# Attention on one core: TensorE takes two score tiles, then the transposes of two tiles, then values

## The reference

```python
scores = jnp.einsum('bqhd,bkhd->bhqk', q, k) * scale
attn = jax.nn.softmax(scores, axis=-1)
out = jnp.einsum('bhqk,bkhd->bqhd', attn, v)
...
x = _layernorm(x + _L0_attn_ref(x, ...))
x = _layernorm(x + _L0_ffn_ref(x, ...))
```

## Time and profile before

| | us |
|---|---|
| median of 3 runs | 987.49 |
| lowest and highest | 984.86, 988.55 |
| the profiled execution | 981.67 |
| its span, first to last instruction | 980.0 |
| TensorE busy in it | 918.8 |
| ScalarE, VectorE, GpSimd busy | 680.4, 633.7, 672.0 |

### The profile page before, as it was taken

One profiled execution on the slowest core, in us unless ns is written; L12 is line 12 of the kernel. 1 busy time (PEld: TensorE's weight loads), 2 busy tenths in 40 slices (PEclk: granted clock), 3 DMA queues, 4 the chain that ended last, 5 costly groups with the idle time before them and its releaser, 6 DMA issues.

```text
span 980.0 us, 17588 instructions
## 1 busy us (share of the span) xinstructions
PE 918.8 (94%) x5110; PEld 637.5 (65%) x5110; DVE 633.7 (65%) x1008; ACT 680.4 (69%) x1140; POOL 672.0 (69%) x503
## 2 busy tenths in 40 slices
PE   6799899999999999979989989999999999998985
PEld 3558666666666666658776866666666666666874
DVE  1665677777776677744457667777777777773455
ACT  3735988888878888851334598888878888875132
POOL 0007788988888989760341778889898988875034
PEclk9999999999999999999999999999999999999998
DMA  9834798888787887999000579888787787889201
GB/s 254 260 156 113 141 167 156 147 152 152 150 155 144 152 152 145 160 177 346 16 25 23 129 140 165 149 156 158 144 159 148 147 152 150 151 155 194 118 1 43
DMA packets 419814, 142.24 MB, mean 145 GB/s; under 512 B 405596, under 2 KB 413616, under 8 KB 418736
## 3 DMA queue, kind: packets, MB, share of 16 engines
q1 hardware_dynamic: 418160, 131.11, 67.8%
q10 hardware_dynamic: 1024, 8.39, 2.2%
q0 software_dynamic: 576, 2.10, 0.6%
HBM read 24.38 MB, written 8.13 MB: 33 GB/s over the span
## 4 chain that ended last, share of the span: by engine, by line
PE 56%; issue 15%; ACT 10%; DVE 9%; POOL 5%; DMA 2%; ACTq 1%; DVEq 1%; POOLq 0%
PE Sa L1054 14%; PE Sb L1054 12%; PE Oa L1083 9%; DVE nmax L774 5%; ACT P_parts L451 3%; POOL P_parts L385 3%; ACT probs_a L552 3%; PE Sb L1107 2%; PE Tb L1065 2%; PE Sa L1107 2%; DMA Wvo_lo<-wvo_low 2%; POOL g_lo L427 2%; PE Ta L1065 1%; PE Ob L1093 1%; ACT PT_hi L451 1%
## 5 line engine op out<-in xcount | busy, mean ns | idle before, releaser
L385 POOL TENSOR_TENSOR P_parts<-probs_a,P_parts 128x768 f16<-128x768 f32 x128 | 211.5, 1652 | 43.3 <-ACT P_parts L451 42.1
L385 POOL TENSOR_TENSOR P_parts<-probs_b,P_parts 128x768 f16<-128x768 f32 x128 | 211.6, 1655 | 36.8 <-ACT P_parts L451 36.6
L774 DVE TENSOR_REDUCE nmax<-Sb 128x1 f32<-128x1024 f32 x128 | 156.8, 1225 | 58.2 <-PE Sb L1054 58.2
L774 DVE TENSOR_REDUCE nmax<-Sa 128x1 f32<-128x1024 f32 x128 | 154.8, 1210 | 37.8 <-PE Sa L1054 37.7
L1083 PE MATMUL Oa<-PT_dma,V_hi 128*64 128x512 f16 x768 | 132.3, 385 | 0.0
L552 ACT ACTIVATE probs_b<-Sa,nmax 128x1024 f32<-128x1024 f32 x64 | 71.3, 1114 | 68.4 <-DVE nmax L777 68.2
L361 POOL TENSOR_TENSOR turned<-qmul 128x1024 f32<-128x1024 f32 x16 | 38.1, 2402 | 104.0 <-DVE qmul L769 104.0
L451 ACT ACTIVATE P_parts<-probs_a 128x768 f16<-128x768 f32 x128 | 107.8, 842 | 0.4 <-DMA PT_dma<-P_parts 0.4
L451 ACT ACTIVATE P_parts<-probs_b 128x768 f16<-128x768 f32 x128 | 107.3, 840 | 0.0
L1054 PE MATMUL Sa<-K_hi,Q_hi 128*128 128x512 f32 x256 | 93.1, 445 | 10.0 <-ACT probs_b L552 9.3
L1054 PE MATMUL Sb<-K_hi,Q_hi 128*128 128x512 f32 x256 | 93.5, 446 | 7.2 <-ACT probs_a L552 4.5
(11 more groups left out here) (293 smaller groups left out, 1946.0 us busy)
## 6 DMA issues: line engine op xcount, KB each, us to landing
QO<-turned SPq DMA_DIRECT2D x64, 128.0 KB, 2.4
TT<-ternary SPq DMA_DIRECT2D x2, 2304.0 KB, 10.8
PT_dma<-P_parts SPq DMA_TRANSPOSE x256, 3.7
ternary<-tern ACTq DMA_DIRECT2D x1, 2304.0 KB, 8.2
wo<-in_L_attn_w_o_dram SPq DMA_DIRECT2D x4, 512.0 KB, 8.5
xq<-in_L_attn_x_dram SPq DMA_DIRECT2D x2, 1024.0 KB, 10.0
wq_high<-Wq_hi ACTq DMA_DIRECT2D x1, 2048.0 KB, 12.8
Wvo_lo<-wvo_low ACTq DMA_DIRECT2D x2, 1024.0 KB, 8.4
```

The source lines that it names most:

```text
L385: nc.gpsimd.tensor_tensor(P_parts[:, n % DEEP, 1, :], probs[n % DEEP][:, KP * P:S], P_parts[:, n % DEEP, 0, :], ALU.subtract).then_inc(par ...
L774: nc.vector.tensor_reduce(nmax[:, n % 4:n % 4 + 1], SS[n % 2][:, :], AX.X, ALU.max, negate=True).then_inc(row_max, 1)
```

## The change

On TensorE, tiles are taken in twos: scores n + 2 and n + 3, transposes n and n + 1, then (where n % 8 is 2) sums_to_rows, then values, two chunks. So the transposes of the even tile and sums_to_rows stand behind the scores of tile n + 3, where they stood ahead of them. Nothing else is changed: what the instructions compute, their number, their semaphores and the lists of the other engines are the same.

```diff
                     t0 = pair * TILES
-                    for n in range(TILES):
-                        if not (last and n >= TILES - 2):
-                            scores(t0 + n + 2, (n + 2) % TILES, pair + (n + 2) // TILES)
-                        transpose_probs(t0 + n, pair * (TILES // 2) + n // 2, n, not (last and n >= TILES - 2))
+                    for n in range(0, TILES, 2):
+                        for i in range(2):
+                            if not (last and n == TILES - 2):
+                                scores(t0 + n + i + 2, (n + i + 2) % TILES, pair + (n + 2) // TILES)
+                        for i in range(2):
+                            transpose_probs(t0 + n + i, pair * (TILES // 2) + n // 2, n + i,
+                                            not (last and n == TILES - 2))
                         if first and n == 8:
                             pe.wait_ge(lat_out, b * 8 * GROUPS + 8 * GROUPS)
                         if not (first and n < 8):
                             if n % 8 == 2:
                                 sums_to_rows(pair * 2 + n // 8 - 1)
-                            if n % 2 == 1:
-                                for k in range(n % 8 - 1, n % 8 + 1):
-                                    values(pair * 2 + n // 8 - 1, 1 - n // 8, k)
+                            for k in range(n % 8, n % 8 + 2):
+                                values(pair * 2 + n // 8 - 1, 1 - n // 8, k)
```

## The result

The changed kernel takes 999.59 us (median of 4 runs, 993.71 to 1003.4), the kernel before beside it 986.17 (4 runs). The ratio is 1.0139, 95% interval 1.0071 to 1.0208: slower, by 13.4 us between the medians, with the size known only to within some 7 us on either side. A second measurement on another occasion, 9 runs against 14, gave 1.0100, 1.0064 to 1.0135. Forecast were 1003.5 us and +16.

The account below looks back on a forecast made before the run. A ring of waits over several engines, not TensorE alone, was taken as the bound. +0.66 - 0.13 = +0.53 us a half, times 30, is 15.9, about 16; on the median 987.49 this gives 1003.5 us, range 991 to 1010.

Parts of the forecast that it names:

- The ring: Attention loop, 8 tiles a half: waits over several engines total 20.80 us; round 6 to round 2 takes 10.28, through the normalisations.
- Round 2 pays 0.66: Round 2, Sb scores to next Sa: transposes (0.22) and sums_to_rows (0.44) no longer fill the exponent wait; 3.25 becomes 3.91 us.
- Round 4 gives back 0.13: Round 4, starting later: its Sb scores no longer wait for the exponent; 4.83 us in place of 4.96.
- First load: Scores right behind scores: the first weight load is hidden if the bank is free early, 1.39 us a tile; held, 1.50.
- Rival 1: Scores behind scores: the load stays open, 0.11 more a half, 19 us in all, 1006.7 us; chance 0.13.
- Rounds 6 and 0: Late transposes there cost nothing, hidden by ScalarE and VectorE; Sa of round 2 still comes 10.28 us after round 6.
- The cover: Rounds 6 and 0: 0.14 us to spare before late transposes show; without it they would cost up to 0.22 a half.
- Which TensorE's order doesn't touch: Round 6 to round 2: the 10.28 us through the normalisations were claimed independent of TensorE's order.
- 30 halves: Halves with sums_to_rows inside the loop, 15 a batch: 30 x 0.53 = 15.9 us.
- 2, faster by a full TensorE: TensorE is the bound; Sb's load hides in all four rounds, 0.11 each, 14 us less, 973.4 us; chance 0.07.
- 3, absorbed: Something else holds round 4 and absorbs round 2's 0.66; within 4.9 us, 987.5 us; chance 0.11.
- 4, a second wait: Late transposes and rows delay PT_hi or row_out, then an exponent; each 0.5 us costs 15, about 1017 us; chance 0.06.

Follow-up runs that it names:

- rows between: Changed kernel, but sums_to_rows put back between the two score tiles of round 2, transposes staying behind them; ratio to the kernel before 1.0056, 5.5 us.
- round 2 old: Changed kernel, but round n % 8 == 2 in the order of the kernel before; ratio to the kernel before 1.0072, 7.1 us.
- the early normalise: Kernel before, with VectorE's normalise moved ahead of transposed_low of a half's last tile; ratio 0.9876, 977.54 against 988.82 us.
- The first two experiments: "rows between", and the kernel before with only sums_to_rows moved behind the odd tile's transposes; ratio to the kernel before 1.0056 each.
- the changed kernel with normalise early: Changed kernel, with VectorE's normalise moved ahead of transposed_low of a half's last tile; ratio to the kernel before 1.0085.

## Why the prediction was right, point by point

The time, the sign and the mechanism came out as forecast. By its steps:

- *The ring.* Right. In the kernel before, Sa of round 6 to Sa of round 2 is 10.28, in the changed one 10.29, in "rows between" and "round 2 old" 10.29, whatever TensorE's order among these; and the early normalise shortened this segment, with 0.07 more in 2a-2b.
- *Round 2 pays 0.66.* Right: 2b-4a went from 3.22 to 3.88. The first two experiments take it apart, 0.22 for the transposes (3.44) and 0.44 for sums_to_rows (3.66).
- *Round 4 gives back 0.13.* Right in mechanism, mis-sized a little: 4.83 forecast and measured (1.50 + 3.33), but the median of the kernel before is 4.99, not the 4.96 of the half that I read, so 0.16 comes back. 0.66 - 0.16 = 0.50 against a forecast of 0.53.
- *First load.* The lower bound was the right one. In the changed kernel, scores right behind scores whose bank is free go from 252.93 to 253.39 in 0.46 us for two matmuls; held ones take 0.57 (258.67 to 259.24 in that timeline). The Sa tiles of rounds 4 and 6, which come behind values, take 0.57 too with nothing held, so the wait is not the only thing that leaves a load open. Rival 1 falls. So does the rule that stands beside it, of the Trainium skill, "TensorE: Matmul & The Clock Gate", section "The mechanism", in the form in which the prediction has it: the trace does not agree that a load overlaps running matmuls only in another row group.
- *Rounds 6 and 0.* Right that they cost nothing here: Sb of round 6 waits (1.89 forecast 1.87), Sb of round 0 does not (1.50), and Sa of round 2 is held by the normalisations. The cover is as thin as said: 0b-2a is 3.47 where TensorE by itself needs 3.33 (4b-6a, the same work), so 0.14 us were to spare, as forecast. What the prediction did not look at is that VectorE's normalise needs the values of round 6, which TensorE's new order makes 0.38 later. "Which TensorE's order doesn't touch" is therefore wrong as a rule: that path had about 0.04 us left, as the changed kernel with normalise early shows, and that it did not bind was luck.
- *30 halves.* 30 x 0.49 = 14.7 us. Forecast were 15.9; the 0.04 a half between them are the 4.96 that should have been 4.99, and rounding. The measured 13.4 and, the second time, 10 us lie below; the intervals of both ratios (7 to 20 and 6 to 13 us) reach down to 6 and the second one ends just short of 14.7. Halves and loops say the change more sharply than medians of executions do, since those also carry the granted clock of the other stages (last section).
- *Rivals.* 2, faster by a full TensorE: Sb does hide its load in rounds 4 and 0, but only the 0.16 of round 4 counts. 3, absorbed: 0.16 of 0.66, no more. 4, a second wait: PT_hi and rden_row follow their exponents at the old distances (261.44 and 261.92 after the exponent at 259.60, against 299.07 and 299.55 after 297.23); none was late.

## What to carry to other kernels

A busy share of 98% does not say that an engine is the bound: look whether its instructions start a constant few hundredths of a microsecond behind another engine's end. Small work that stands ahead of a waiting instruction is free up to the length of that wait, and the same work behind it costs its full price; so before like work is put together, ask which wait each piece was filling. And walk the ring of waits once around, segment by segment: an edit pays only in the segments that its engine is in, two edits in one segment need not add (0.37 and 0.04 here for the same edit), and a segment that seems to belong to another engine has a path through yours that may be only 0.04 us shorter.

## What was not expected of the hardware

Two executions of the very same changed kernel, profiled, differ by 9.7 us in span (992.0 and 1001.7), while their halves agree (21.31 and 21.32). The rows of the first score matmuls, changed kernel and then its second profile, show that 6.8 us of it lie before the attention loop has begun: it starts at 99.5 in the one and at 106.3 in the other, and 801.7 and 802.4 us later comes the last Sa tile.

```profile
L1054 PE MATMUL Sa<-K_hi,Q_hi x256: 387/402/504, 99.5 to 901.2; 128*128 128x512 f32 x128
```

```profile
L1054 PE MATMUL Sa<-K_hi,Q_hi x256: 389/402/504, 106.3 to 908.7; 128*128 128x512 f32 x128
```

The windows of the first 98 us in the same two profiles show what differs: TensorE is busy equally long, but its granted clock is 0.97 in the first and 0.93 in the second (the number ahead of the last two), and fewer instructions are through (x374 against x344).

```profile
0.00:98.00 98.00, 83.36 (x374) 55.54 (x375) 49.95 (x69) 48.73 (x98) 20.83 (x21) 0.97 0.65 193
```

```profile
0.00:98.00 98.00, 83.31 (x344) 53.20 (x345) 48.31 (x67) 44.52 (x91) 14.69 (x18) 0.93 0.63 188
```

It is so in all nine profiles of this text: where the clock of these 98 us is 0.97 or 0.98, in five of them, the loop begins at 98.0 to 101.9 us; where it is 0.91 or 0.93, in four, at 103.5 to 106.3. An estimate from these figures is that 0.04 of 98 us is 3.9 us of TensorE's full-speed time, so the clock accounts for over half of the 6.8 us by itself; what the rest is stays open, and nothing here shows why the clock falls in one execution and not in another.

The times without a profile go the same way. Of the nine executions in the second measurement of the changed kernel, four had a mean granted clock of 0.981 or 0.982 and took 999.35 to 1003.46 us, five had 0.989 to 0.992 and took 991.92 to 996.15. The kernel before had on average the lower clock there, 0.9835 against 0.9861, which makes the ratio of 1.0100 too low. At 0.982 on both sides it is 1003.3 (median of three) against 988.9 (two), 14.4 us, near the 14.7 of the loops. So a median of executions compares two kernels only as well as their clocks agree; the 6.8 us are half the size of the change.
